# A second phase over 16 sequences: the final scaling is issued one sequence later, and the lower parts of the transposes one sequence sooner

## The chip, the cores and the metric

The kernel runs on one core of one Trainium2 chip. The metric is the device time of one execution in microseconds (us), the median of several runs. TensorE (PE), VectorE (DVE), ScalarE (ACT), GpSimd (POOL) and SyncE (SP, which here only issues DMAs) each work through their own list of instructions in order; semaphores are the only link between the lists.

## The reference

The input is 16 sequences of 512 tokens with 256 channels. What is computed is, cut to what matters:

```python
x = layernorm(x + attention(x))          # sliding window of 128, 16 heads, with a slope per head
c = in_c                                 # one state row per batch row, (512, 256)
for xt in x:                             # a recurrence over the 16 sequences
    f, i = sigmoid(xt @ wf.T + c @ uf.T + bf), sigmoid(xt @ wi.T + c @ ui.T + bi)
    g = tanh(xt @ wc.T + c @ uc.T + bc)
    c = f * c + i * g
h = tanh(x @ wo.T + c_final @ uo.T + bo) # for every sequence, with the LAST state
out = layernorm(x + h)
```

Since `h` needs the state after the last sequence, nothing of `h` for any sequence can be finished before the recurrence has ended.

## The kernel before, in words

**First phase.** Lines 202 to 1306 hold, engine by engine, a pipeline over sequences: attention, first layer norm, recurrence. Its result for each sequence (call it x1, 512 KB) is stored to a DRAM tensor `x1_dram`. The change does not touch it.

**Second phase.** It runs over 16 sequences t = 0 to 15 (in the order `ORDER`, the last sequence first). Each x1 is read back from DRAM into one of four buffers, `ring[t % 4]` (in the profile these carry the names of what they held earlier: `y`, `xt_raw`, `o_tok`, `x_res`). What each engine does for a sequence, in its own order:

- SP, `move(u)`: wait until the sum of sequence u is made, since then `ring[u % 4]` is free; issue the load of x1 for u + 4 (line 301); wait until sequence u is scaled (`fin2`); issue the store of the result (line 308). Then comes `move(u + 1)`. So the load for u + 4 stands in SP's list behind the store for u - 1.
- PE: `transpose2(u + 1)`, 8 transposes of the next x1 into two banks (line 1206), then `product_wo(u)`, 24 matmuls with Wo (line 1306), then `add_cu(u)`, 4 matmuls that add the part of the state (line 1316). `transpose2` waits for its load (`x1_in`). `product_wo(u)` waits for the tanh of u - 2 (its banks) and for the lower parts of u.
- ACT, `hidden(t)`: `hi2(t + 1)`, two copies that round the transposes of t + 1 to the upper parts (line 568); the two tanh of t (line 643); `layernorm2(t - 1)`, four activations of 128x256 that scale and shift sequence t - 1 (line 652), each raising `fin2`.
- DVE, `finish(t)`: `lo2(t + 1)`, two operations for the lower parts of the transposes (helper, line 669), which wait for the upper ones; the sum z = h + x1 (line 894); four times `bn_stats` (897) and four times `bn_aggr` (902).
- POOL, `second(t)`: four small operations from the moments to the scale and the shift (lines 403, 404, 406, 408). It raises `sh2`, which `layernorm2` waits for.

The order is written out by hand; there is no planner. The sums z go to four buffers `z_ring[t % 4]`, and z of t waits until the store of t - 4 has landed (`out_sem`).

In the first rounds, `lo2(1)` and `lo2(2)` stand ahead of the loop, and `finish(0)` and `finish(1)` hold none. `hi2(3)` stands in `hidden(2)`.

Of the kernel before, what the change touches and what calls it, by code (L numbers as in the profile page):

```python
# [5 lines left out]
B, S, E = 16, 512, 256  # L6
# [34 lines left out]
def build(nc, x, xt, w_in, w_out, w_gates, u_gates, b_gates, w_o, u_o, b_o, in_c, q_rows, k_rows, q_slopes, out):  # L41
# [3 lines left out]
    with ctx:  # L45
# [162 lines left out]
        def steps(eng, step, last=B):  # L208


            for t in range(B):
                step(t, t // 4, t % 4)
# [201 lines left out]
        def _(act):  # L414
# [146 lines left out]
            def hi2(u):  # L561
                if u == 1:
                    act.wait_ge(op_ready, 2 * B)
                else:
                    act.wait_ge(wo_done, u - 1)
                for c in range(KC):
                    act.wait_ge(t2_ready, 2 * (u - 1) + c + 1)
                    sc.activation(parts2[u % 2][:, 0, c, :], T2[u % 2][c][:, :], ACT.Copy).then_inc(t2hi, 1)  # L568
# [67 lines left out]
            def hidden(t, rnd, i):  # L636
                if 2 < t + 1 < B:
                    hi2(t + 1)
                if t >= 2:
                    act.wait_ge(z_done, t - 1)  # L640
                for a in range(2):
                    act.wait_ge(o2_ready, 2 * t + (a + 1))
                    sc.activation(h_ring[i % 2][:, a, :], banks[4 + 2 * (i % 2) + a][:, :], ACT.Tanh).then_inc(h_done, 1)  # L643
                if t >= 1:
                    layernorm2(t - 1, i - 1)

            def layernorm2(t, i):

                act.wait_ge(sh2, t + 1)
                z = z_ring[i % 4]  # L650
                for n in range(NB):
                    sc.activation(z[:, n, :], z[:, n, :], ACT.Identity, bias=shift[:, i % 2, n:n + 1],  # L652
                                  scale=rstd[:, i % 2, n:n + 1]).then_inc(fin2, 1)

            hi2(2)
            for a in range(2):
                act.wait_ge(cu_sum, a + 1)
                sc.activation(cu[:, 0, 2 * a:2 * a + 2, :], x_hidden[:, a, :].rearrange("p (n e) -> p n e", n=2), ACT.Copy).then_inc(cuhi_done, 1)
            steps(act, hidden)
            layernorm2(B - 1, B - 1)  # L660


        @block.vector
        def _(dve):
            ve = nc.vector

            def minus_hi(out_, in_, hi, scale=1.0):

                return ve.scalar_tensor_tensor(out_, in_, scale, hi.bitcast(F32), op0=ALU.mult, op1=ALU.subtract)  # L669
# [145 lines left out]
            def lo2(u):  # L815
                for c in range(KC):
                    dve.wait_ge(t2hi, 2 * (u - 1) + c + 1)
                    minus_hi(parts2[u % 2][:, 1, c, :], T2[u % 2][c][:, :], parts2[u % 2][:, 0, c, :]).then_inc(t2lo, 1)
# [67 lines left out]

            def finish(t, rnd, i):

                if 2 < t + 1 < B:
                    lo2(t + 1)  # L890
                if t >= 4:
                    dve.wait_ge(out_sem[i], 16 * rnd)
                dve.wait_ge(h_done, 2 * t + 2)
                ve.tensor_tensor(z_ring[i], h_ring[i % 2].rearrange("p a (n e) -> p (a n) e", e=E), ring[i], ALU.add).then_inc(z_done, 1)  # L894
                dve.wait_ge(z_done, t + 1)
                for n in range(NB):
                    ve.bn_stats(stats[:, n, :], z_ring[i][:, n, :]).then_inc(st2, 1)  # L897
                if t >= 2:
                    dve.wait_ge(sh2, t - 1)
                for n in range(NB):  # L900
                    dve.wait_ge(st2, 4 * t + (n + 1))
                    ve.bn_aggr(mean_var[:, i % 2, n, :], stats[:, n, :]).then_inc(mv2, 1)
# [7 lines left out]
            for a in range(2):  # L910
                dve.wait_ge(cuhi_done, a + 1)
                minus_hi(cu[:, 1, 2 * a:2 * a + 2, :], x_hidden[:, a, :].rearrange("p (n e) -> p n e", n=2),
                         cu[:, 0, 2 * a:2 * a + 2, :]).then_inc(culo_done, 1)
            steps(dve, finish)


# [472 lines left out]
```

## Time and profile before

| | us |
|---|---|
| median of 3 runs | 988.29 (987.64 to 988.79) |
| profiled execution, its own time | 991.27 |
| its span, first to last instruction | 989.2 |
| granted TensorE clock, mean over the span | 0.955 of full speed |
| busy: PE, DVE, ACT, POOL | 908.1, 713.5, 573.6, 412.1 |

The span is what the trace's times count in; the profiled execution took 2.07 us more than its span, and 2.98 us more than the median of the unprofiled runs. The second phase is the last tenth of the span. Times in the rows below are from the span's start. A row of the timeline gives start, duration, engine, line, the operation with out<-in, the number of merged instructions and, in brackets, the idle time of the engine before them with what ended it.

### The profile page before, as it was taken

Reading aid. Unit: us, or ns where it says so; the run is one execution under the profiler, and the core shown is the slowest. Engines: PE = TensorE matmul, PEld = TensorE weight load, DVE = VectorE, ACT = ScalarE, POOL = GpSimd, SP = SyncE. Lnnn points to the kernel's source line nnn. Section 1 sums busy time; section 2 is a strip of 40 time slices with the busy share of each in tenths; the row PEclk is TensorE's granted clock in tenths of the full one; section 3 lists DMA queues with packets and bytes.
Section 4 is the critical chain, followed back from the end, with each engine's and each line's share of the span. In section 5 each row is a group of like instructions: output and inputs, shape, how many; then the busy total and the mean of one; then the engine's idle time right before and its main releaser. Section 6 shows DMA issues by size and latency. Waiting matters only on the chain. (4 is left out here: it accounts for less than half of the span.)

```text
span 989.2 us, 25966 instructions
## 1 busy us (share of the span) xinstructions
PE 908.1 (92%) x9492; PEld 749.0 (76%) x9492; DVE 713.5 (72%) x2793; ACT 573.6 (58%) x1165; POOL 412.1 (42%) x687
## 2 busy tenths in 40 slices
PE   3587879999999999999999999999999999898994
PEld 2365668888888888888888888888888877677884
DVE  7665676877777787878787878787878673346785
ACT  5044455565657575756565656565757564435776
POOL 6133333444444444545353535353535352201443
PEclk8577889999999999999999999999999999998998
DMA  7734454544444454545445545455444410202673
GB/s 255 173 112 120 126 140 141 136 144 132 148 130 151 127 151 125 150 128 151 128 150 127 154 126 151 129 150 131 147 113 145 125 46 22 86 22 71 187 215 125
DMA packets 92478, 130.82 MB, mean 132 GB/s; under 512 B 12096, under 2 KB 46528, under 8 KB 92352
## 3 DMA queue, kind: packets, MB, share of 16 engines
q1 hardware_dynamic: 92080, 128.90, 45.7%
q8 instruction: 76, 1.25, 0.5%
q14 instruction: 50, 0.41, 0.1%
q10 hardware_dynamic: 272, 0.26, 0.1%
HBM read 78.78 MB, written 49.81 MB: 130 GB/s over the span
## 5 line engine op out<-in xcount | busy, mean ns | idle before, releaser
L697 DVE CUSTOM_DVE_ANT_0 bank<-bank,mask 128x256 f32<-128x256 f32 (+1 forms) x1024 | 369.5, 423 | 132.7 <-PE bank L959 130.9
L454 ACT ACTIVATE Pt<-bank 128x512 f32<-128x512 f32 (+1 forms) x512 | 248.4, 536 | 193.5 <-PE bank L980 193.4
L352 POOL TENSOR_SCALAR_AFFINE_SELECT Pt<-Pt 128x512 f32<-128x512 f32 x256 | 171.0, 668 | 401.5 <-ACT Pt L454 401.5
L959 PE MATMUL bank<-Ks,Qs 59*128 59x256 f32 (+1 forms) x1024 | 148.8, 319 | 46.6 <-DVE max_q L697 30.2
L959 PEld LDWEIGHTS bank<-Ks,Qs 59*128 59x128 f32 x1024 | 107.8, 192 | 88.3 <-DVE max_q L697 41.8
L354 POOL TENSOR_SCALAR_AFFINE_SELECT Pt<-Pt 128x384 f32<-128x384 f32 x256 | 146.0, 570 | 0.0
L697 DVE DVE_READ_ACCUMULATOR2_ANT max_q<- 128x1 f32 x1024 | 145.2, 142 | 0.0
L994 PE MATMUL bank<-Pt,Vp 128*32 128x256 f32 (+1 forms) x2048 | 130.0, 374 | 0.0
L940 PE MATMUL bank<-x1T,Wg 64*128 64x512 f32 x960 | 127.9, 398 | 1.1 <-DVE o_tok L711 1.1
L940 PE MATMUL bank<-cT,Ug 64*128 64x512 f32 x960 | 125.7, 393 | 0.0
L980 PE MATMUL bank<-Qs,Ks 60*128 60x256 f32 (+1 forms) x1024 | 111.3, 271 | 0.0
L994 PEld LDWEIGHTS bank<-Pt,Vp 128*32 128x32 f32 x2048 | 81.2, 115 | 31.2 <-issue 6.9
L940 PEld LDWEIGHTS bank<-cT,Ug 64*128 64x128 f32 x960 | 89.1, 184 | 18.2
L940 PEld LDWEIGHTS bank<-x1T,Wg 64*128 64x128 f32 x960 | 87.0, 185 | 19.2 <-DVE o_tok L711 1.4
L980 PEld LDWEIGHTS bank<-Qs,Ks 60*128 60x128 f32 x1024 | 94.9, 193 | 1.9 <-issue 1.3
L465 ACT ACTIVATE ctx_raw<-bank 128x512 f32<-128x512 f32 x64 | 38.3, 598 | 55.8 <-PE bank L1002 51.2
L492 ACT ACTIVATE gate<-bank,bias_half 128x512 f32<-128x512 f32 x64 | 42.4, 685 | 38.7 <-PE bank L940 23.8
L928 PE MATMUL bank<-xT,Win 128*128 128x512 f32 x204 | 54.2, 418 | 8.6 <-DVE Win L669 8.6
L940 PE MATMUL bank<-Win,xT 64*128 64x256 f32 x768 | 55.7, 287 | 0.0
L928 PEld LDWEIGHTS bank<-xT,Win 128*128 128x128 f32 x204 | 39.7, 201 | 17.1 <-DVE Win L669 8.6
L669 DVE SCALAR_TENSOR_TENSOR qk_parts<-bank,qk_parts 128x512 fp32r<-128x512 f32 x64 | 42.5, 685 | 13.7 <-ACT qk_parts L437 13.7
L940 PEld LDWEIGHTS bank<-Win,xT 64*128 64x128 f32 x768 | 51.9, 193 | 0.0
(111 smaller groups left out, 1332.7 us busy)
## 6 DMA issues: line engine op xcount, KB each, us to landing
parts_dram<-qk_parts SPq DMA_DIRECT2D x128, 256.0 KB
Qs<-parts_dram SPq DMA_DIRECT2D x128, 128.0 KB, 2.7
Ks<-parts_dram SPq DMA_DIRECT2D x128, 128.0 KB, 2.8
xt_raw<-in_xt SPq DMA_DIRECT2D x16, 512.0 KB, 4.3
Qs<-parts_dram SPq DMA_DIRECT2D x128, 64.0 KB, 2.7
Ks<-parts_dram SPq DMA_DIRECT2D x128, 64.0 KB, 2.8
x_res<-in_x SPq DMA_DIRECT2D x16, 512.0 KB, 3.9
result<-Pt SPq DMA_DIRECT2D x16, 512.0 KB, 3.1
```

Of the source, the lines that this page charges most:

```text
L352: gp.affine_select(out=p4[:, :, 0:128], in_=p4[:, :, 0:128], compare_op=ALU.is_ge, fill=0.0, base=0, pattern=[[0, 4], [1, 128]], channel_m ...
L354: gp.affine_select(out=p4[:, 0:3, 128:256], in_=p4[:, 0:3, 128:256], compare_op=ALU.is_ge, fill=0.0, base=0, pattern=[[0, 3], [-1, 128]], ...
L454: sc.activation(probabilities(g, 2 * pair + odd)[:, S * a:S * a + n], SC[odd][:, 0:n], ACT.Exp).then_inc(exp_done, 1)
L465: sc.activation(ctx_raw[:, :], bank[:, :], ACT.Copy).then_inc(ctx_done, 1)
L492: ins = sc.activation(gate[:, k if k == 3 else which, :], bank[:, :], ACT.Tanh, bias=bias_half[:, which, j:j + 1], scale=0.5)
L669: return ve.scalar_tensor_tensor(out_, in_, scale, hi.bitcast(F32), op0=ALU.mult, op1=ALU.subtract)
L697: ins = ve.tensor_tensor_reduce(out=raw, in0=raw, in1=mask[:, keys], scale=1.0, scalar=MASKED, op0=ALU.add, op1=ALU.max, accum_out=max_q[: ...
L928: ins = te.matmul(out_, w, m, start=(first and n == 0), stop=(last and n == len(todo) - 1))
L940: ins = te.matmul(out_, w(r), m(r), start=(turn == 0 and opens and n == 0), stop=final, skip_group_check=True)
L959: ins = te.matmul(MX[odd][:, 256 * (n % 2):256 * (n % 2) + 256][:, keys], Qs[rows, 2 * g + pair, n * WIN:(n + 1) * WIN], Ks[rows, 2 * g + ...
L980: ins = te.matmul(SC[odd][:, 256 * (j % 2):256 * (j % 2) + width], Ks[rows, 2 * g + pair, j * WIN:(j + 1) * WIN], Qs[rows, 2 * g + pair, j ...
L994: ins = te.matmul(bank[32 * hh:32 * hh + 32, j * WIN:j * WIN + width], Vp[:, j, PITCH * h:PITCH * h + 32], probabilities(g, hh)[:, 256 * j ...
```

## The change

In ACT's list `layernorm2` of a sequence moves from behind the tanh of the next sequence to behind the tanh of the next but one. At the end of the loop two of them follow instead of one. In DVE's list `lo2` of a sequence moves one `finish` sooner: `finish(t)` begins with `lo2(t + 2)` instead of `lo2(t + 1)`. The number of instructions, their shapes, the semaphores' counts and the lists of PE, POOL and SP stay as they are.

```diff
@@ ACT, hidden(t)
-                if t >= 1:
-                    layernorm2(t - 1, i - 1)
+                if t >= 2:
+                    layernorm2(t - 2, i - 2)
...
             steps(act, hidden)
+            layernorm2(B - 2, B - 2)
             layernorm2(B - 1, B - 1)
@@ DVE, finish(t)
-                if 2 < t + 1 < B:
-                    lo2(t + 1)
+                if 0 < t and t + 2 < B:
+                    lo2(t + 2)
```

## Rows read from the trace of the kernel before

**Rows 1.** The page: TensorE's busy tenths and its granted clock, 40 slices.

```profile
PE   3587879999999999999999999999999999898994
PEclk8577889999999999999999999999999999998998
```

**Rows 2.** Chain of waits, 927 to 938: start, us, what.

```profile
927.82 0.98 ACT gate L643 x2
...
928.89 1.24 DVE Pt L894
...
931.99 0.24 POOL var_eps L403
...
933.74 1.19 POOL shift L408
```

**Rows 3.** Timeline of the steady stretch, 931 to 941.

```profile
932.42 1.04 PEld L1206 LDWEIGHTS bank<-ident,y 128*128 128x128 f32 x8
932.44 1.09 ACT L643 ACTIVATE c<-bank 128x512 f32<-128x512 f32 x2 [0.73 <-PE bank L1316]
...
933.42 2.89 PEld L1306 LDWEIGHTS bank<-Wo,oT 128*128 128x128 f32 x24
...
934.95 2.08 ACT L652 ACTIVATE Pt<-Pt,shift,rstd 128x256 f32<-128x256 f32 x4 [1.43 <-POOL shift L408]
...
936.25 0.77 PEld L1316 LDWEIGHTS bank<-qk_parts,ident_r 128*128 128x128 f32 x4
...
937.07 1.03 PEld L1206 LDWEIGHTS bank<-ident,xt_raw 128*128 128x128 f32 x8
...
937.89 1.06 ACT L643 ACTIVATE gate<-bank 128x512 f32<-128x512 f32 x2
...
938.85 2.08 ACT L652 ACTIVATE Pt<-Pt,shift,rstd 128x256 f32<-128x256 f32 x4
938.95 2.89 PEld L1306 LDWEIGHTS bank<-Wo,x1T 128*128 128x128 f32 x24 [0.85 <-ACT gate L643]
```

**Rows 4.** Timeline, SP's issues of one store and the load behind it.

```profile
926.89 0.38 SPq L308 DMA_DIRECT2D result<-Pt  x1
...
927.31 0.51 SPq L301 DMA_DIRECT2D y<-x_dram  x1
```

**Rows 5.** Landing times of the loads of line 301; DMA issues, the stores (us last).

```profile
DMA to landing us min/median/max: 3.9/4.7/5.0
...
result<-Pt SPq DMA_DIRECT2D x16, 512.0 KB, 3.1
```

**Rows 6.** Timeline of the phase's first rounds, 901 to 917.

```profile
901.66 1.09 ACT L643 ACTIVATE gate<-bank 128x512 f32<-128x512 f32 x2
...
903.07 0.36 SPq L301 DMA_DIRECT2D y<-x_dram  x1
...
905.57 1.09 PE L1316 MATMUL bank<-qk_parts,ident_r 128*128 128x512 f32 x4
...
907.01 1.09 PE L1206 MATMUL bank<-ident,y 128*128 128x128 f32 x8 [0.34 <-DMA y<-x_dram]
...
911.72 5.39 PE L1306 MATMUL bank<-Wo,oT 128*128 128x256 f32 x24 [3.62 <-ACT c L643]
```

**Rows 7.** Timeline of the phase's end: last transposes, last tanh.

```profile
967.51 1.02 PEld L1206 LDWEIGHTS bank<-ident,x_res 128*128 128x128 f32 x8
...
977.51 1.05 ACT L643 ACTIVATE gate<-bank 128x512 f32<-128x512 f32 x2
```

**Rows 8.** Windows of 2 us: length, PE busy, PEld, DVE, ACT, POOL, clock, DMA share, GB/s.

```profile
806.00:808.00 2.00, 1.10 (x10) 0.75 (x12) 1.37 (x8) 1.39 (x4) 0.94 (x2) 0.92 0.00 0
808.00:810.00 2.00, 2.00 (x20) 1.54 (x24) 1.57 (x8) 0.34 (x2) 1.24 (x3) 0.50 0.00 0
...
912.00:914.00 2.00, 2.00 (x11) 2.00 (x11) 1.97 (x4) 2.00 (x5) 0.00 (x0) 0.50 0.88 270
938.00:940.00 2.00, 1.36 (x12) 1.15 (x10) 1.77 (x3) 2.00 (x5) 0.59 (x2) 1.00 0.98 281
```

## Prediction

> **What bounds the kernel now.** I read the page first. TensorE is busy nine tenths or more nearly everywhere, at full clock, with a dip only in the last tenth [rows 1]. The change touches only that last tenth, so the question is what sets the pace there. Next I read the chain of waits in a steady stretch. It does not run through TensorE. It goes tanh, sum, statistics, POOL's four small steps, scaling, then the next tanh but one [rows 2]. The timeline puts numbers on it: a tanh starts at 927.8 and the tanh two sequences later at 937.89, so 10.1 us for two sequences, 5.07 each [rows 2, 3]. ACT sits idle 1.43 us ahead of one scaling, waiting for POOL's shift, and TensorE loses 0.85 us once per two sequences [rows 3].
>
> TensorE's own floor comes from the same rows. Transposes start at 932.42, product at 933.42, `add_cu` at 936.25, the next transposes at 937.07. That is 1.00 + 2.83 + 0.82 = 4.65 us per sequence [rows 3]. Between 5.07 and 4.65 lie 0.42 us per sequence that a change of order alone can win.
>
> The third thing to read is SP's list. The store of u - 1 is issued when its scaling ends, and the load for u + 4 follows 0.42 us later [rows 4]. A load lands 4.7 us after its issue (3.9 to 5.0 over all 12) [rows 5]. In this example: issue 927.31, landing 932.0, and the transposes of that buffer start at 932.42 [rows 3, 4]. The margin is 0.4 us. This loop waits for nothing yet, but it is nearly as tight as the one on the chain.
>
> **The change part by part.**
>
> 1. *Scaling behind the next tanh but one.* ACT executes as many instructions as before. The wait for POOL's shift (1.43 us per two sequences) goes. The shift starts 3.10 us (sum to `var_eps`) + 1.75 us after the sum begins and takes up to 1.19 us, so it is ready 6.0 us after it [rows 2]; the scaling now comes more than nine us after the sum. What is moved with it is `fin2`. SP's store of u - 1, and the load for u + 4 queued behind it, now wait for the tanh of u + 1 instead of the tanh of u: one whole sequence later. TensorE needs the load no later than before. So at the old pace the margin of 0.4 us turns into a shortage of 3 to 4.7 us (5.07 later, less the 1.43 us that the scaling no longer waits).
>
> 2. *The new loop.* I follow one load, from a tanh to the tanh two sequences on. Tanh start to scaling start 0.96 (937.89 to 938.85); scaling 2.08; to the store's issue 0.03; to the load's issue 0.42; landing 4.7; to the first transpose about 0.03 [rows 3 to 5]. From the transposes' start to the tanh behind them: 1.00 + 2.83 + 0.11 to the first matmul of `add_cu` + 0.73 until ACT may start = 4.67 [rows 3]. Sum: 8.22 + 4.67 = 12.9 us per two sequences, 6.44 each, against 5.07. There are two such loops, one over odd and one over even sequences, side by side; 2 x 4.65 = 9.3 of 12.9 us is TensorE's work, so it is idle 3.6 us per pair.
>
> 3. *Lower parts one sequence sooner.* The operations cost the same. `lo2` of u is ready one sequence earlier, 1.9 us after `hi2` starts. The sum z now stands behind `lo2(t + 2)`, so behind the transposes of t + 2: it starts some 2.6 us after these begin. Who waits for z: POOL (covered above), the tanh of t + 2 and the load for t + 4, which are all held longer by the new loop. Where it pays is the start of the phase. There TensorE was idle 3.62 us ahead of `product_wo(3)`, because `lo2(3)` waited behind ACT's first scaling, and that product then ran at the lower clock: 5.39 us instead of 3.05 [rows 6]. This stall goes: `hi2(3)` can run once the tanh of 1 is done, 902.7, and `lo2(3)` behind the statistics of 0, which end near 904.7, and the product follows the transposes of 4 at 908.0. Late next is the load for 5.
>
> 4. *Start.* The tanh of 2 may start 0.73 behind `add_cu(2)` (905.57), 906.3. The shift of 0 starts near 906.6; the sum of 1 (905.9 to 907.2) runs beside it, and as in rows 2 the shift then ends with it, 907.2. Scaling of 0: 907.25 to 909.33; store, then load for 5 issued at 909.8, landing 914.5. Transposes of 5 start there (TensorE free since 911.9: 2.6 us idle). In the even loop the transposes of 6 start near 919.8, those of 8 near 932.6. In the odd one: 914.5, 927.35, 940.2, 953.1, 966.0, 978.9 for 15 [rows 6].
>
> 5. *End.* The transposes of 15 started at 967.51 and start at 978.9. Behind them: product 14, `add_cu` 14, product 15, `add_cu` 15, tanh of 15: 1.00 + 2.83 + 0.82 + 2.83 + 0.11 + 0.73 = 8.3, so 987.2 instead of 977.51 [rows 3, 7]. After the last tanh nothing changes: two earlier scalings (4.2 us) fit between it and the last shift, 1.2 us of tanh and then 3.10 + 1.75 + 0.2 = 5.1 us [rows 2].
>
> Sum without any change of clock: +9.7 us on the profiled span (989.2 to 998.9), 998.0 on the scale of the median of 988.29 (2.98 below the profiled execution's 991.27).
>
> 6. *The clock.* Here the trace of before shows both ends, not the case itself. An idle of 0.85 us in a pair leaves the clock at 1.00; 3.6 us of idle from 908 on is followed by 0.50, half of full speed and so 1.2 GHz; and a stretch near 807, with TensorE busy only half the time, is followed by 0.50 as well [rows 6, 8]. The new stalls are 2.6 us once and then about 3 us ahead of every odd load (a small rest ahead of the even one), six long ones. Cost of one: nothing at the lower end, 5.39 - 3.05 = 2.3 us at the upper [rows 6], more only if `add_cu` and the transposes are hit too (up to 4.65 us, the whole of one sequence at half speed). They lie much nearer to the 3.6 us row. I take 2.2 us for four of the six, 8.8 us; the cost is in the loop and not hidden, because the load is issued behind the tanh. Bounds: 0 and 6 x 2.3 = 14.
>
> Forecast: 988.3 + 9.7 + 8.8 = 1006.8 us, slower by 1.9%.
>
> The DMA's price has a second source. The Trainium skill, page "DMA: Bandwidth & Descriptors", section "Anatomy of one DMA", fits a DMA (on the GpSimd path) as about 2.0 us plus bytes over 436,000 per us; for 512 KB that is an estimate of 3.2 us. The trace disagrees for these loads (4.7 us, behind a store of the same size) and agrees for the stores (3.1) [rows 5]. With 3.2 the new loop would close in 11.4 us per pair and the whole would come out near 989, no change; that is rival C.
>
> **The rivals.**
>
> A. *Late loads, clock stays up.* 998.0 us. For it: each new idle stretch is shorter than the one of 3.6 us. Against: the stretch near 807 fell with much less idle in one piece [rows 8].
>
> B. *Clock at 0.50 nearly throughout.* TensorE's part of the loop doubles each time: 6 x 3.9 = 23 us, 1021 us. Against: the clock came back after a full product at half speed (clock 0.50 at 912, 1.00 again by the steady stretch) [rows 8].
>
> C. *Loads land fast enough.* Let L be the landing time. The last tanh starts at 909.8 + L + 5 x (8.19 + L) + 8.3, which is 977.5 for L = 3.1. That is the point from which it decides: under 3.1 the change is faster, down to TensorE's floor, where the transposes of 5 start at 911.9, those of 15 at 958.4, and the time is about 978. For it: the stores land in 3.1 [rows 5]. Against: 12 loads, none under 3.9, and even a lone one took 3.9 [rows 5, 6]. With 3.9 throughout it would be 993.
>
> D. *The scaling is not what holds SP.* If the load were in another place of SP's list, the time would be the 978 of C. The list's order (store of u - 1, then load for u + 4) is seen in every pair of issues [rows 4], so I give it almost nothing; it counts with C.
>
> **How the numbers follow.** Forecast (late loads, clock falls after most long stalls, 1001 to 1014) 0.59; A with its surroundings (995 to 1001) 0.22; B (over 1014) 0.08; L near 3.9 (989.5 to 995) 0.05; C and D: within 0.2% 0.02, faster 0.04. The likeliest is 1006.8. The range 996 to 1014 leaves out B and everything under 996, about 2 in 10. Faster by over 0.2% 0.04; within 0.2%, about what a measurement tells from no change, 0.02; slower 0.94.
>
> **What would show it.** In the trace of after, transposes (line 1206) must wait for the DMA `<-x_dram` in nearly every sequence from 5 on, some 3.6 us per pair. The idle time ahead of the scaling (line 652) by POOL's shift must be gone, the stall ahead of `product_wo(3)` too. The load's issue must stand about 0.4 us behind the end of a scaling, and two tanh of the same parity must be 12.9 us apart or more. The clock must show 0.50 behind some of the stalls; if it never does, the time is A's. The prediction is wrong if the transposes don't wait for a DMA.

## The result, and the profile after

The changed kernel takes 1008.84 us (median of 4 runs, 1005.75 to 1010.04) against 988.19 us (4 runs, 987.64 to 988.79): a ratio of 1.0184, 95% interval 1.016 to 1.0207. It is 20.6 us slower. The profiled execution took 1009.01 us, with a span of 1007.0 us and a mean granted clock of 0.949.

The page shows where to look: ahead of the last slice TensorE's busy tenths fall to 7 and 8, and the clock ends at 8, 8 and 7, where before both were at 8 or 9 [rows 1].

```profile
PE   3587889999999999999999999999999898997784
PEclk9677879999999999999999999999999999999887
```

The next view is the list of waits over the second phase, longest first (engine, line, releaser: us in total, times, longest). From line 660 on the lines have moved by one. Before, the list had 16.6 us of line 652 waiting for POOL's shift, in nine waits, and hardly any wait for a load. The first fence is that line of before, the second the list after.

```profile
ACT Pt L652 <- POOL shift L408: 16.6, 9, 4.9
```

```profile
POOL var_eps L403 <- DVE mean_var L903: 92.5, 15, 28.8
ACT c L643 <- PE bank L1317: 26.6, 8, 4.6
...
PEld bank L1207 <- DMA xt_raw<-x_dram: 11.2, 3, 4.6
PEld bank L1207 <- DMA x_res<-x_dram: 10.4, 3, 3.7
...
ACT Pt L652 <- POOL shift L408: 1.2, 1, 1.2
...
PEld bank L1207 <- DMA o_tok<-x_dram: 1.0, 1, 1.0
```

POOL's line stands first and costs nothing: it is an engine with little to do. The wait for the shift is down to one of 1.2 us, for the last sequence (1001.48); in the loop there is none, as forecast. In its place the weight loads of the transposes wait for the loads from DRAM, 23.3 us in all over 8 waits. The chain of waits, 931 to 947 (start, us, what), is the loop that replaced that of [rows 2]:

```profile
931.38 0.86 ACT c L643 x2
932.24 0.11 issue
932.35 2.08 ACT Pt L652 x4
934.43 0.02 issue
934.44 0.38 SPq L308
934.82 0.04 issue
934.87 5.62 DMA xt_raw<-x_dram
940.48 0.04 issue
940.53 1.97 PE bank L1207 x8
942.50 4.41 PE bank L1307 x24
```

Tanh, scaling, store's issue, load's issue and landing, transposes, product. The timeline gives the same place from TensorE's side, with the idle time ahead in brackets; it answers to [rows 3]:

```profile
925.33 1.91 PE L1207 MATMUL bank<-ident,x_res 128*128 128x128 f32 x8 [2.56 <-DMA x_res<-x_dram]
...
931.58 1.04 PE L1207 MATMUL bank<-ident,y 128*128 128x128 f32 x8
...
934.87 0.51 SPq L301 DMA_DIRECT2D xt_raw<-x_dram  x1
...
940.53 1.97 PE L1207 MATMUL bank<-ident,xt_raw 128*128 128x128 f32 x8 [4.15 <-DMA xt_raw<-x_dram]
...
942.15 4.75 PE L1307 MATMUL bank<-Wo,x1T 128*128 128x256 f32 x24
```

From the transposes of 7 (925.33) to those of 9 (940.53) are 15.2 us, against 10.2 before (927.12 to 937.30). The stall is 4.15 us ahead of one odd sequence (9) and 2.56 us ahead of the one before it (7); ahead of the even one between them there is none (931.58). And behind the stall the engine is slow: 8 transposes take 1.97 us instead of 1.04, the product 4.75 instead of 3.05. The windows (length, PE, PEld, DVE, ACT, POOL busy, clock, DMA share, GB/s) show the clock at 0.50 there, that is 1.2 GHz, and at 1.00 a few us later:

```profile
936.00:940.00 4.00, 0.38 (x2) 0.00 (x0) 3.04 (x10) 3.04 (x6) 0.62 (x3) 0.89 0.73 212
940.00:942.00 2.00, 1.47 (x7) 1.47 (x8) 0.00 (x0) 0.26 (x1) 1.08 (x2) 0.50 0.98 272
942.00:944.00 2.00, 2.00 (x11) 2.00 (x10) 1.53 (x3) 0.93 (x2) 0.00 (x0) 0.50 0.75 250
...
947.50:949.50 2.00, 2.00 (x19) 1.91 (x18) 0.00 (x0) 2.00 (x5) 1.21 (x2) 1.00 0.00 0
```

The loads themselves hardly changed: 3.9, 4.7, 6.0 us to landing (least, median, longest) against [rows 5]. The one in the chain above took 5.6 us; the three odd ones behind it took 4.7, and the stalls ahead of their transposes were 3.2 to 3.3 us instead of 4.15.

**A better ruler.** The first phase is the same code in all kernels here, but it does not end at the same time in each profile. The product of sequence 1 (line 1306 of the kernel before, 1307 after) started at these times, first before and then after:

```profile
897.20 2.99 PE L1306 MATMUL bank<-Wo,oT 128*128 128x256 f32 x24
```

```profile
895.48 2.88 PE L1307 MATMUL bank<-Wo,oT 128*128 128x256 f32 x24
```

So the length of the second phase, from there to the span's end, is 92.0 us before (989.2 - 897.2) and 111.5 us after (1007.0 - 895.5): 19.5 us longer. I give this length for every experiment beside the ratio; it is good to some 0.1 us, since the first matmul of such a row can be missing. Each length comes from one profile; only the changed kernel with the load ahead of the store was profiled twice.

| kernel | ratio to before (95%) | second phase, us |
|---|---|---|
| before | 1 | 92.0 |
| changed | 1.0184 (1.016 to 1.0207) | 111.5 |
| changed, load ahead of the store | 0.9919 (0.9896 to 0.9942), again 0.9927 (0.9902 to 0.9953) | 84.6, 84.8 |
| before, load ahead of the store | 0.9989 (0.9966 to 1.0012) | 92.0 |
| scaling moved alone | 1.0214 (1.0183 to 1.0244) | 112.9 |
| lower parts moved alone | 1.0472 (1.0442 to 1.0501) | 139.3 |
| changed, filler matmuls | 1.0084 (1.005 to 1.0117) | 101.3 |
| changed, load after scaling, ahead of store | 1.0035 (1.0015 to 1.0055) | 97.7 |
| scaling moved, load ahead of the store | 0.9921 (0.9899 to 0.9943) | 82.4 |

In the sessions of the experiments the kernel before ran at a median of 990.8 to 991.1 us, so ratios are compared, not times.

### The profile page after: what moved, and what is told of

The parts are those of the page before. It is cut to its first block and busy times, and to the rows that moved or that the text cites. A ratio compares the mean times of both kernels' runs of the same rounds, so it can differ in the third digit from the quotient of the medians.

```text
span 1007.0 us, 25966 instructions
## 1 busy us (share of the span) xinstructions
PE 915.8 (91%) x9492; PEld 757.8 (75%) x9492; DVE 714.5 (71%) x2793; ACT 574.7 (57%) x1165; POOL 403.6 (40%) x687
## 5 line engine op out<-in xcount | busy, mean ns | idle before, releaser
L981 PE MATMUL bank<-Qs,Ks 60*128 60x256 f32 (+1 forms) x1024 | 111.5, 270 | 0.0
```

The source lines that it names most:

```text
L981: ins = te.matmul(SC[odd][:, 256 * (j % 2):256 * (j % 2) + width], Ks[rows, 2 * g + pair, j * WIN:(j + 1) * WIN], Qs[rows, 2 * g + pair, j ...
```

## The experiments

**1. The changed kernel with the load ahead of the store.**

```diff
             def move(u, rnd, i):
                 if u + 4 < B:
                     sp.wait_ge(z_done, u + 1)
                     load(u + 4, i)
-                sp.wait_ge(fin2, 4 * u + 4)
-                sp.dma_start(out[ORDER[u]]..., z_ring[i]).then_inc(out_sem[i], 16)
+                if u >= 1:
+                    store(u - 1)    # the same wait and DMA, for u - 1
...
             steps(sp, move, B - 4)
+            store(B - 1)
```

> The changed kernel, with one edit: in SP's list the load for u + 4 stands ahead of the store of u - 1 instead of behind it, so it waits only until the sum of u is made. Theory (the load is held by the scaling, through the store ahead of it in SP's list): the waits of the transposes for a DMA go, TensorE's floor of 4.65 us per sequence and the gain at the phase's start come through, and the time is 976 to 980 us. The load is then issued 3.9 us behind the start of the transposes of u + 2 and has 9.3 us until those of u + 4 begin, enough for a landing of 4.7. Rival 1 (the sums z, which now stand behind the lower parts of t + 2, are what is late): moving the load helps little, 1000 us or more. Rival 2 (once the loads are in time, POOL's shift falls beside the next sum, is held to about 6 us, and the scaling waits again): 980 to 985 us, with idle time of ACT ahead of the scaling.

Measured: 982.53 us where the kernel before took 991.02, so 8.5 us less (976 to 980 against 988.3, that is 8 to 12 less, were expected), and a second phase of 84.6 us. One edit of SP's list turns 1.0184 into 0.9919. The cause named by the theory holds and its first rival falls. The second rival holds in part: the saving is at the low end of the theory's, the time itself lies in this rival's range, and the timeline still has small waits, for the DMA and for POOL's shift.

```profile
923.04 1.08 POOL L413 TENSOR_TENSOR shift<-minus_mean,rstd 128x4 f32<-128x4 f32 x1
...
923.36 1.09 PE L1212 MATMUL bank<-ident,y 128*128 128x128 f32 x8 [0.26 <-DMA y<-x_dram]
...
924.16 2.08 ACT L657 ACTIVATE Pt<-Pt,shift,rstd 128x256 f32<-128x256 f32 x4 [0.35 <-POOL shift L413]
```

From the transposes of 7 (918.30) to those of 11 (937.79) are 19.5 us, 4.87 per sequence and not 4.65. A second run of the same kernel, to set it beside experiment 7:

> The changed kernel with the load ahead of the store, a second time, beside the version without the moved lower parts: as in its first run, a ratio of 0.990 to 0.994 to the kernel before; it decides nothing but the difference between the two.

Measured 982.61 us, a ratio of 0.9927, phase 84.8 us. Its first phase ended 6 us later than in the first run's profile (product of sequence 1 at 899.99 instead of 893.83), though the code is the same.

**2. The kernel before with the load ahead of the store.** The same edit of `move`.

> The kernel before, with the same edit of SP's list alone (the load ahead of the store of the sequence before it). Theory: before, the loads just arrived in time (0.4 us of margin) and the pace was set by sum, statistics, shift and scaling, so the time stays at 988 us, within 1 us. Rival (the loads already cost something before, or the transfer behind the store took DMA bandwidth that mattered): 2 us or more faster.

Measured: 0.9989 (0.9966 to 1.0012), second phase 92.0 us, the same as before to a tenth. The loads now had 3.9 us to landing in the median, with more time to spare, and nothing came of it. So before the change the loads were in time and not the bound; the change made them late. The interval alone would still allow 3 us; the length of the phase does not.

**3. The scaling moved alone.**

```diff
                 if 2 < t + 1 < B:
                     lo2(t + 1)      # as before; ACT as in the changed kernel
```

> Half of the change: the scaling stands behind the next tanh but one, the lower parts stay where they were. Theory (the late load is made by the moved scaling alone): the same loop of 12.9 us per pair plus the clock's share, transposes wait for the DMA in every pair, 1006 to 1012 us; the stall ahead of the product of sequence 3 is much shorter than 3.6 us already, since the first scaling is out of ACT's way. Rival (the moved lower parts hold the sum and with it the load): without them the time is near the kernel before, 980 to 990 us.

Measured: 1012.02 us, 1.0214, second phase 112.9 us. The late loads come from the moved scaling. The stall ahead of the product of sequence 3 was 0.84 us here. Both halves together are 1.4 us shorter in the phase than this one; in total time the two can't be told apart (their intervals overlap).

**4. The lower parts moved alone.**

```diff
-                if 2 < t + 1 < B:
-                    lo2(t + 1)
+                if 0 < t and t + 2 < B:
+                    lo2(t + 2)      # ACT as in the kernel before
```

> The other half: the lower parts one sequence sooner, the scaling behind the next tanh as before. Theory: a closed loop over one sequence appears. The sum of t stands behind the lower parts of t + 2, these behind the upper parts of t + 2 on ACT, these behind the scaling of t - 1, and this behind the shift of t - 1, so behind the sum of t - 1: 4.9 to the shift's start + 0.2 + 2.0 for the scaling + 0.6 + 1.3 = 9.0 us per sequence instead of 5.07, over some 13 sequences: about 1040 us, 1030 to 1050. Rival (the lower parts can move freely, their place costs nothing): 982 to 990 us.

Measured: 1038.36 us, 1.0472, second phase 139.3 us. The timeline shows the closed loop; one turn of it, from sum to sum:

```profile
946.40 1.22 DVE L894 TENSOR_TENSOR Pt<-gate,xt_raw 128x1024 f32<-128x1024 f32 x1
...
951.22 0.20 POOL L408 TENSOR_TENSOR shift<-minus_mean,rstd 128x4 f32<-128x4 f32 x1
951.45 2.08 ACT L652 ACTIVATE Pt<-Pt,shift,rstd 128x256 f32<-128x256 f32 x4 [4.85 <-POOL shift L408]
...
953.44 1.05 ACT L568 ACTIVATE x1T<-bank 128x512 fp32r<-128x512 f32 x2
...
954.04 1.29 DVE L669 SCALAR_TENSOR_TENSOR x1T<-bank,x1T 128x512 fp32r<-128x512 f32 x2 [4.71 <-ACT x1T L568]
...
955.25 1.22 DVE L894 TENSOR_TENSOR Pt<-c,o_tok 128x1024 f32<-128x1024 f32 x1
```

946.40 to 955.25 is 8.85 us; expected was 9.0. An order of instructions on DVE that carries no data dependence with it can still close a loop through two other engines. In the changed kernel the moved scaling opens this loop, since the scaling ahead of the upper parts of t + 2 is then that of t - 2.

**5. Filler matmuls.** Nothing is computed with them; the transposes overwrite what they write.

```diff
             def transpose2(u):
-                pe.wait_ge(x1_in[u % 4], 16 * ((u + 3) // 4))
...
+                if u >= 5 and u % 2 == 1:
+                    for n in range(20):
+                        te.matmul(T2[u % 2][0][:, 0:E], Wo[:, 0, 0, 0:128], Wo[:, 0, 1, :], start=True, stop=True)
+                pe.wait_ge(x1_in[u % 4], 16 * ((u + 3) // 4))
```

> The changed kernel; ahead of its wait for the load of every odd sequence from 5 on, TensorE also runs 20 extra matmuls (128x256 into the bank that the transposes then overwrite, about 0.12 us each, 2.4 us in all), which fill most of a stall of about 3 us. Nothing is computed with them. Theory (about half of the loss is the clock that falls to 1.2 GHz after the stalls): with the stalls filled the clock stays at full speed, pairs take 12.9 us instead of 14.7, and the time falls by 8 to 12 us, to 1.009 to 1.013 of the kernel before, although TensorE does 120 matmuls more. Rival (the slower products are not caused by the idle time, or the waits are longer for another reason): the ratio stays at 1.018 or rises by up to 6 x 2.4 = 14 us.

Measured: 1.0084, second phase 101.3 us, 10.2 us shorter than the changed kernel's with 120 matmuls more. The saving is within the 8 to 12 us expected; the ratio lies just below the 1.009 to 1.013. The same stretch in windows, and one filled stall:

```profile
936.00:940.00 4.00, 3.02 (x24) 2.72 (x23) 2.37 (x9) 3.04 (x6) 1.29 (x3) 1.00 0.59 156
940.00:942.00 2.00, 2.00 (x19) 2.00 (x20) 0.75 (x2) 1.09 (x2) 0.41 (x2) 1.00 0.95 283
```

```profile
936.34 2.55 PE L1204 MATMUL bank<-Wo 128*128 128x256 f32 x20
...
939.87 1.09 PE L1210 MATMUL bank<-ident,xt_raw 128*128 128x128 f32 x8 [0.98 <-DMA xt_raw<-x_dram]
```

The clock stays at 1.00, and the transposes of the odd sequences from 5 to 15 start 12.8 us apart (913.67 to 977.66, five pairs), the 12.9 of the loop at full clock. This splits the loss in two: 9.3 us that stay at full clock (101.3 - 92.0) and 10.2 us of clock. The 9.3 are a balance: against the kernel before, the five pairs from the transposes of 5 to those of 15 are 14.1 us longer (64.0 instead of the 49.9 from 917.87 to 967.74), the start up to the transposes of 5 is 3.3 us shorter, since the old stall and its slow product are gone, and the end is 1.5 us shorter.

**6. The load behind the scaling, but ahead of the store.**

```diff
                 if u + 4 < B:
                     sp.wait_ge(z_done, u + 1)
+                    if u >= 1:
+                        sp.wait_ge(fin2, 4 * u)
                     load(u + 4, i)
+                if u >= 1:
+                    store(u - 1)
```

> The changed kernel; SP still waits for the scaling of u - 1 ahead of the load for u + 4, but issues this load ahead of the store instead of behind it. Theory (the loop is scaling, issue, landing, transposes, product, tanh): the loop loses 0.42 us of issue and up to 0.8 of the landing (4.7 behind a store, 3.9 alone), 1.2 us per pair of about 14.7: 5 pairs and the first load, 6 to 8 us less than the changed kernel, a ratio of 1.010 to 1.013 to the kernel before. Rival (the load's place behind the store, not the wait for the scaling, is what costs): close to the time with the load ahead of both, a ratio of 0.99.

Measured: 1.0035, second phase 97.7 us, 13.8 us shorter than the changed kernel's: outside what I expected, and nowhere near the rival. The loads land in 4.3 us in the median of all 12, the odd ones from 5 to 13 in 4.1 to 4.2, and pairs of odd transposes are 11.7 us apart (911.92, 923.71, 935.39, 947.12, 958.85). From the 12.9 of the loop go 0.42 of issue and 0.6 of landing, which would leave 11.9.

```profile
923.71 1.09 PE L1214 MATMUL bank<-ident,x_res 128*128 128x128 f32 x8 [1.35 <-DMA x_res<-x_dram]
...
925.09 0.36 SPq L301 DMA_DIRECT2D y<-x_dram  x1
...
929.62 1.09 PE L1214 MATMUL bank<-ident,y 128*128 128x128 f32 x8 [1.07 <-DMA y<-x_dram]
```

What I missed is that I took the 1.2 us off 14.7, a pair with its slow clock in it. The shorter loop leaves stalls of 0.3 to 1.75 us, and after none of these did the clock fall. It fell once, behind the one of 2.09 us, and the pair with it took 13.2 us:

```profile
964.00:966.00 2.00, 0.24 (x2) 0.24 (x3) 1.83 (x9) 2.00 (x5) 0.00 (x0) 1.00 1.05 372
966.00:968.00 2.00, 2.00 (x13) 2.00 (x12) 0.83 (x2) 1.53 (x3) 1.69 (x4) 0.59 0.32 85
```

So a saving of 1.2 us per pair also gave back the clock's share. It is a second witness beside experiment 5. The experiment also splits the 26.9 us between the changed kernel and experiment 1 (111.5 - 84.6): 13.8 come with the load's place ahead of the store, the other 13.1 with its release from the scaling, the clock's share included in both.

**7. The scaling moved and the load ahead of the store, the lower parts as before.** Experiments 3 and 1 combined.

> The moved scaling with the load ahead of the store in SP's list, and the lower parts where they were before the change. Theory (with the load freed, the sum z standing behind the lower parts of t + 2 is what still makes loads land 0.3 to 0.6 us late and POOL's shift collide): the sum starts right behind its tanh, some 4 us sooner, so no transposes from 5 on wait for a DMA and the pitch falls from about 4.85 to TensorE's 4.65 to 4.7 us; against that stand 0.8 us of stall ahead of the product of sequence 3. In all 0.5 to 2 us faster than with the lower parts moved, a ratio of 0.989 to 0.991 to the kernel before. Rival (the lower parts sooner give the product slack that it needs): 1 to 3 us slower than with them, with TensorE idle ahead of line 1306's products.

Measured: 983.52 us, 0.9921 (0.9899 to 0.9943), second phase 82.4 us, 2.2 to 2.4 us shorter than with the lower parts moved. The ratio lies above the 0.989 to 0.991 expected, though the phase gained more than the 0.5 to 2 us expected: the totals don't show the gain. In total time the two can't be told apart (0.9921 and 0.9927, measured side by side); the first phase ended at 901.01 and 899.99 in their profiles. Within the phase the mechanism is plain:

```profile
926.54 2.07 ACT L657 ACTIVATE Pt<-Pt,shift,rstd 128x256 f32<-128x256 f32 x4
...
926.57 3.05 PE L1312 MATMUL bank<-Wo,x1T 128*128 128x256 f32 x24
...
930.39 1.03 PE L1212 MATMUL bank<-ident,y 128*128 128x128 f32 x8
...
935.01 1.04 PE L1212 MATMUL bank<-ident,xt_raw 128*128 128x128 f32 x8
```

No bracket of idle time stands in any of these lines. The transposes follow each other at 4.62 us (930.39 to 935.01), from those of 5 to those of 15 (916.53 to 962.74): TensorE's floor. Two short waits for the lower parts are left, 0.82 us ahead of the product of 3 and 0.46 us ahead of that of 15.

## Why the prediction was right

**What bounds the kernel before.** Right. Experiment 2 shows that the loads did not bind before; experiment 7 shows that TensorE's floor of 4.65 us is real (4.62).

**The new loop.** Right in its mechanism, shown by experiments 1 and 3: freeing the load from the scaling removes the loss, moving the scaling alone makes it. Its length at full clock, 12.9 us per pair, was 12.8 in experiment 5. My walk put the transposes of 5 and 15 at 914.5 and 978.9, 64.4 us apart; experiment 5 has 64.0, the changed kernel 71.7 (912.52 to 984.22), the clock's share included. The change without the clock's share was put at 9.7 us; 9.3 measured. One sign failed: the transposes should have waited for a load in nearly every sequence from 5 on, and from 7 on only the odd ones did.

**The start.** Right: the product of 3 started at 906.00, 0.84 us behind the first transpose of 4 (905.16), without the old stall [rows 6], and took 3.08 us at full clock. The first stall for a load was 2.50 us, 2.6 forecast.

**The clock.** The size came out near, 8.8 forecast and 10.2 measured, but the picture behind it was off. I had a stall of about 3 us ahead of the odd load and a small rest ahead of the even one. In fact the slower half of the pair pushed the even sequence until it started right behind the odd one, so its stall vanished and the odd one grew, to 4.15 us once and 3.2 to 3.3 us three times. The first stall (2.50 us) was followed by no slow product (3.05 us), the next five all were (3.77 to 5.07 us). From the first transpose to the first matmul of `add_cu` these five took 5.2 to 6.5 us against 3.73 behind the first stall (912.52 to 916.25), 10.0 us in all. So it was five of six at 2.0 us where I had four of six at 2.2: a count too low and a price too high that partly offset each other, so the nearness is luck in part. I had put the price on the product, with the transposes as a mere possibility. Measured, 6.5 of the 10.0 us stand in the products and 3.5 in the transposes ahead of them (1.6 to 2.0 us instead of 1.0 to 1.1).

**The lower parts.** I wrote that every engine waiting for the sum is held longer by the new loop anyway. True there, but the moved lower parts are not free: with the loads freed they cost 2.2 to 2.4 us of the phase (experiments 1 and 7), and without the moved scaling 47 us (experiment 4). That their safety hangs on the moved scaling was not in the prediction.

**The rivals.** A falls since the clock fell, B since it was back at 1.00 in every pair; with the clock held up, experiment 5 came to 1.0084, 996.5 us on the scale of 988.2, near A's 998.0. For C the break-even landing was 3.1 us; the loads took 3.9 to 6.0. D falls with experiment 1, where an edit of SP's list alone took the loss away. The Trainium skill's fit for a DMA (page "DMA: Bandwidth & Descriptors", section "Anatomy of one DMA", for the GpSimd path) gives an estimate of 3.2 us here. It does not hold for these loads, which SP issues: even ahead of the store in the list they took 3.6 us at the least and 3.9 in the median (experiment 1).

**What stays open.** The total came out 20.6 us above before, the second phase 19.5. The first phase is the same code, yet the product of sequence 1 started between 893.8 and 901.0 us in the ten profiles; nothing here explains why, and it hides differences of 2 us in the totals. When the clock falls is open too: its fall behind one stall and not behind another of the same length (below) is not explained by the stall alone.

## What to carry to other kernels

When work is moved later on one engine, follow its semaphore into every queue: here a DMA store waited for it, and a load that had nothing to do with it stood behind the store in the same list. Margins of the loads against their use belong beside the chain of waits: here the loop with 0.4 us to spare was the next bound. And put the load ahead of the store: with that one edit the same idea gains 0.8% instead of losing 1.8%, and it gains as much without the moved lower parts.

## What the runs showed of the hardware

- TensorE's clock fell to 0.50 behind an idle stretch of 2.09 us (experiment 6), of 2.56 us and more (the changed kernel), and of 2.20 and 2.44 us (experiment 4, whose products behind them took 4.60 and 4.29 us). It did not fall behind one of 2.50 us (the changed kernel), behind three of 2.45 and 2.46 us (experiment 4, products of 2.96 to 3.06 us), or behind those of up to 1.75 us in experiment 6. So in these traces the length of one stall does not tell. Extra matmuls of no use in the wait kept it at 1.00 and made the phase 10.2 us shorter.
- A load of 512 KB took 3.9 us in the median where it stood ahead of the store in SP's list (experiments 1 and 2), 4.7 right behind a store of the same size, and up to 6.0 in the changed kernel. The load of 9 there took 0.9 us longer than those of 11, 13 and 15 (5.62 against 4.69 to 4.74), and the stall behind it was 0.9 us longer (4.15 against 3.24 to 3.26). A store took 3.1 us ahead of a load, and 5.1 in the median right behind one (experiment 6).
- POOL's shift (128x4) took 0.20 us alone and 1.05 to 1.12 us when it began 0.16 to 0.23 us behind the start of DVE's sum of two SBUF tensors; it ended with the sum. In experiment 7 it was so in all nine rounds from 922 to 960 and cost nothing, since the scaling came later.
